# Feed-forward layers: GpSimd makes a block's scale one tile later, and ScalarE makes the shifted copies for the next layer

## The reference, cut to what matters

```python
h = shift_token(x)                     # channels 64..127 come from the token before
q, k, v = jnp.split(h @ wqkv, 3, axis=-1)      # 8 heads of 64
q = l2norm(q) * qs;  k = l2norm(k) * ksc
q, k = rotary_xpos(q, k)
o = local_attention(q, k, v)           # windows of 64, each sees itself and the one before
x = x + o @ wo
h = shift_token(x)
h = (h - h.mean(-1)) / jnp.sqrt(h.var(-1) + 1e-05) * lg + lb
a, g = jnp.split(h @ w1 + b1, 2, axis=-1)
x = x + (a * jax.nn.gelu(g, approximate=False)) @ w2 + b2
```

## Time and profile before

| | |
|---|---|
| median of 3 runs | 1290.07 us (1289.85 to 1290.78) |
| profiled execution, its own time | 1292.57 us |
| its span, first to last instruction | 1290.8 us |
| mean granted TensorE clock | 0.870 |
| busy: TensorE, VectorE, ScalarE, GpSimd | 79%, 60%, 41%, 32% |
| layer 0: attention and feed-forward | about 938 to 1077 us of the span |
| layer 1: projection; attention and feed-forward | about 1077 to 1143; 1145 to 1284 us |

### The profile page before, as it was taken

One profiled execution on the slowest core, in us unless ns is written; L12 is line 12 of the kernel. 1 busy time (PEld: TensorE's weight loads), 2 busy tenths in 40 slices (PEclk: granted clock), 3 DMA queues, 4 the chain that ended last, 5 costly groups with the idle time before them and its releaser, 6 DMA issues.

```text
span 1290.8 us, 20116 instructions
## 1 busy us (share of the span) xinstructions
PE 1026.0 (79%) x7980; PEld 692.3 (54%) x7980; DVE 774.5 (60%) x1349; ACT 529.7 (41%) x1231; POOL 418.0 (32%) x488
## 2 busy tenths in 40 slices
PE   6895876858545189999999777769889789979887
PEld 3563654636423167878787652334456534546643
DVE  2574574654827534646464668969756557956644
ACT  4646555356123311222212060026686514767732
POOL 0724403324106500000000125439843434954420
PEclk9976967669666589999999988979899899979989
DMA  3307135063144374334631210000111210012101
GB/s 94 73 7 143 32 62 109 6 100 71 23 78 197 66 139 98 98 97 75 120 68 29 92 66 1 0 1 0 34 35 39 58 65 26 1 34 51 43 9 33
DMA packets 60479, 76.50 MB, mean 59 GB/s; under 512 B 37500, under 2 KB 41992, under 8 KB 58632
## 3 DMA queue, kind: packets, MB, share of 16 engines
q1 hardware_dynamic: 60396, 75.36, 25.8%
HBM read 52.87 MB, written 1.51 MB: 42 GB/s over the span
## 4 chain that ended last, share of the span: by engine, by line
PE 51%; DVE 16%; POOL 14%; ACT 5%; SPq 5%; DMA 4%; issue 4%; POOLq 0%; DVEq 0%
PE psum L1189 7%; PE psum L1191 6%; PE psum L1190 6%; POOL rest L1426 3%; POOL rest L1416 3%; POOL rest L1422 2%; PE psum L693 2%; PE psum L1670 2%; SPq L1012 2%; POOL rest L1452 2%; DVE main L506 2%; SPq L1018 2%; PE psum L1716 2%; PE psum L1663 2%; DMA rest<-share_d 2%
## 5 line engine op out<-in xcount | busy, mean ns | idle before, releaser
L406 POOL TENSOR_TENSOR kept<-kept 128x8 f32<-128x8 f32 x8 | 1.6, 202 | 401.5 <-DVE kept L383 401.5
L1375 ACT ACTIVATE rest<-psum,main 128x128 f32<-128x128 f32 x256 | 113.3, 482 | 11.6 <-POOL main L1437 8.9
L1036 ACT ACTIVATE x_high<-main 128x512 fp32r<-128x512 f32 x48 | 30.3, 633 | 199.4 <-DVE main L1110 199.4
L1189 PE MATMUL psum<-x_high,w_low 128*128 128x512 f32 x192 | 76.9, 400 | 20.1 <-DVE x_low L1115 20.1
L1452 POOL TENSOR_TENSOR rest<-rest,main 128x512 f32<-128x512 f32 x64 | 65.4, 1042 | 34.6 <-DVE main L1522 34.6
L1189 PE MATMUL psum<-hid_high,w_low 128*128 128x512 f32 x192 | 75.6, 394 | 0.7 <-DVE main L1134 0.7
L1190 PE MATMUL psum<-x_low,w_high 128*128 128x512 f32 x192 | 76.2, 397 | 0.0
L1191 PE MATMUL psum<-x_high,w_high 128*128 128x512 f32 x192 | 76.1, 396 | 0.0
L1190 PE MATMUL psum<-hid_low,w_high 128*128 128x512 f32 x192 | 74.8, 389 | 0.0
L1191 PE MATMUL psum<-hid_high,w_high 128*128 128x512 f32 x192 | 74.7, 389 | 0.0
L1110 DVE TENSOR_TENSOR main<-kept,rest 128x512 f32<-128x512 f32 x48 | 33.1, 690 | 68.1 <-PE psum L1191 43.8
(11 more groups left out here) (316 smaller groups left out, 2841.2 us busy)
## 6 DMA issues: line engine op xcount, KB each, us to landing
rest<-share_d SPq DMA_DIRECT2D x4, 3072.0 KB, 21.4
rest<-share_d SPq DMA_DIRECT2D x4, 2304.0 KB, 20.4
main<-main SPq DMA_DIRECT2D x32, 256.0 KB, 5.2
main<-k_pad SPq DMA_DIRECT2D x16, 512.0 KB, 7.5
rest<-main SPq DMA_DIRECT2D x32, 256.0 KB, 3.5
main<-w_dram SPq DMA_DIRECT2D x2, 3072.0 KB, 14.0
main<-rest SPq DMA_DIRECT2D x32, 128.0 KB, 4.4
rest<-tables_dram SPq DMA_DIRECT2D x2, 2048.0 KB, 8.7
```

What stands on the lines that cost most here:

```text
L1189: T.matmul(dst, w_small, x_large, start=first, stop=False)
L1375: last = A.activation(probs[:, p, 4 * r + m, :], bank[2 * p + r][:, m * P:(m + 1) * P], ACT.Exp, scale=row_scale[:, c, r, m:m + 1], bias=r ...
```

## The change

Two edits, which meet at no semaphore:

- **GpSimd**: `scales(b)` of blocks 0, 1 and 2 is made in iteration 4b+7 in place of 4b+6, behind the weights of tile 4b+7 and the bias of tile 4b+9. Both layers, 6 places. The scale of block 3 stays where it was, at the end.
- **The shifted copies after the feed-forward of layer 0** (4 blocks, 2 copies each and one column of zeros) are made by ScalarE, from a wait on `ff_x`. VectorE's memset becomes a ScalarE copy of a zero column. Blocks 0 and 1 are put between two gelus, one block behind; blocks 2 and 3 stand ahead of ScalarE's first squares of layer 1. VectorE waits for `ff_x` now only in the last layer and once at the end.

```diff
+                def shift(b):
+                    act.wait_ge(sem("ff_x"), L * BLOCKS + b + 1)
+                    first, to = 512 * b, max(512 * b, 1)
+                    if b == 0:
+                        A.activation(sT[HEAD_DIM:P, 0:1], turn_mark[HEAD_DIM:P, 0:1], ACT.Copy)
+                    A.activation(sT[0:HEAD_DIM, first:first + 512], hT[0:HEAD_DIM, first:first + 512], ACT.Copy)
+                    A.activation(sT[HEAD_DIM:P, to:first + 512], hT[HEAD_DIM:P, to - 1:first + 511], ACT.Copy).then_inc(sem("ff_s"), 1)
+
+                more = L + 1 < DEPTH
                 gelu(0, 2)
                 for b in range(1, BLOCKS):
-                    for i in range(N_FF):
-                        gelu(b, i)
+                    gelu(b, 0)
+                    gelu(b, 1)
+                    if more and b >= 2:
+                        shift(b - 2)
+                    gelu(b, 2)
+                if more:
+                    shift(BLOCKS - 2)
+                    shift(BLOCKS - 1)
...
-                if c % 4 == 2 and c > 2:
+                if c % 4 == 3 and c > 3:
                     scales(c // 4 - 1)
...
-                    dve.wait_ge(sem("ff_x"), L * BLOCKS + b + 1)
-                    if L + 1 < DEPTH:
-                        shift(b)
-                    else:
+                    if L + 1 == DEPTH:
+                        dve.wait_ge(sem("ff_x"), L * BLOCKS + b + 1)
                         V.scalar_tensor_tensor(xT[:, sl], hT[:, sl], gate[:, 11:12], xT[:, sl], ALU.mult, ALU.add).then_inc(sem("x_s4"), 1)
...
                 fed(BLOCKS - 1)
+                dve.wait_ge(sem("ff_x"), L * BLOCKS + BLOCKS)
                 dve.sem_inc(sem("ff_w_free"), 1)
```

## The result

The changed kernel takes 1272.01 us, the median of 4 runs (1267.82 to 1273.43); the kernel before takes 1290.42 us in the same comparison (1289.85 to 1295.06, 4 runs). The ratio is 0.9856, 95% interval 0.9831 to 0.988. The forecast was 1268 us, in a range of 1264 to 1276; 18.4 us were gained where 22.1 had been summed up.

What follows compares the result with a forecast made beforehand. No engine is busy throughout; a chain of waits through VectorE, GpSimd and TensorE was taken to bound the stretch changed. Terms 7.5 + 9.6 + 5.3 - 0.3 = 22.1 us, from 1290.07 to 1268 us; range 1264 to 1276.

Steps and rivals of the forecast that it cites:

- tile 7, layer 0 and 1: Attention: earlier weights let the normalisation and TensorE's transposes back come 2.1 us earlier in layer 0, 1.65 in layer 1.
- tile 11, layer 0 and 1: Attention: the gain of tile 7 was to repeat, 2.1 us in layer 0 and 1.65 in layer 1.
- tile 15, layer 0 and 1: Attention: weights 2.6 us earlier and TensorE's clock staying at 2.4 GHz, 4.95 us in layer 0, 4.6 in layer 1.
- copies of block 0: Layer 0's feed-forward: without VectorE's two copies TensorE goes on at once with block 2 at full clock, 5.3 us.
- layer 1 begins later: Block 3: ScalarE's copies delay its first square of layer 1, 0.3 us lost, up to 1.2.
- rival (a): Clock falls anyway: at tile 15 and block 2, 1274 us; at tiles 7 and 11 of layer 0 alone, 1271; chance 0.20.
- The rule against it: Feed-forward copies: VectorE is faster and not saturated, so edit 2 gives nothing or a small loss, sum 17 us.
- Rival (c): Feed-forward: moving copies gains nothing, as GpSimd holds VectorE's next instruction instead; 16.8 us gained, 1273 us; chance 0.08.
- Rival (b): Tiles 7 and 11: the late scale takes back the 7.5 us, leaving 14.6 us gained, 1275.5 us; chance 0.08.
- Rival (d): Six moved scales: 1.2 GHz through two tiles behind each, up to 8 us more per place, 1316 us; chance 0.03.
- Rival (e): Next tile's weights wait for something else the timeline hides: no measurable effect, 1290 us; chance 0.03.
- the two signs of being wrong: Attention: the normalisation does not start earlier, or stretches at clock 0.50 stand behind the scales.

Runs made afterwards that it cites:

- the normalisation first: Changed kernel with GpSimd's scale ahead of the bias and, at tiles 7 and 11, VectorE's normalisation ahead of copies and reciprocal: 1265.24 us.
- the scores first: Changed kernel with TensorE's transposes back of blocks 0 and 1 one step later, behind the scores of tile 10 (14): 1257.9 us.
- tables-later: Kernel before, with GpSimd's four products on the tables held back until block 0's copies are done: ratio 0.9981.
- copies alone: Kernel before with only the shifted copies moved to ScalarE, the scales left in their old place: ratio 0.9976.
- late at tile 15 alone: Changed kernel with the scales of blocks 0 and 1 back at tiles 6 and 10, block 2's still late: ratio 0.9891 to the kernel before.

## Why the prediction was right

By the ruler, term by term, in us gained:

| term | forecast | measured |
|---|---|---|
| tile 7, layer 0 and 1 | 2.1 + 1.65 | 2.10 + 1.65 |
| tile 11, layer 0 and 1 | 2.1 + 1.65 | 0.53 + 0.08 |
| tile 15, layer 0 and 1 | 4.95 + 4.6 | 5.10 + 5.38 |
| copies of block 0 | 5.3 | 5.37 |
| layer 1 begins later | -0.3 | -0.37 |
| sum | 22.1 | 19.8 |

- **The mechanism** was as told: the weights start behind their reciprocal, and TensorE's wait moves to the transposes back and is 1.9 to 2.0 us long (2 had been said). Waits for the weights fell to 5.8 us (6 said).
- **Tile 11 is the step that failed.** "Tile 11 repeats it" took for granted that the clock there would be as at tile 7. It fell behind the new wait, and 1.57 us went in each layer: the size that rival (a) had put on one fall (1.6), at places that it named only for layer 0. With one such fall in each layer the sum would have been 18.9 us. The two runs that shorten the wait give this loss back: in layer 0 the normalisation first gains 1.6 us more at tile 11 than at tile 7, the scores first 2.2 us more. Over tiles 7 and 11 of both layers in all ten profiles, the clock fell at 19 of the 28 waits of 1.9 to 2.3 us and at none of the 12 waits under 1 us. It fell at none of the 14 waits of 1.25 us at tile 15 either. So in these runs the fall came with the long wait alone, but not with every long wait; why the same wait at tile 7 does no harm stays open.
- **Tile 15** gave 0.9 us more than reckoned, 0.78 of it in layer 1. Of these, 0.63 had been gained before r14: behind it TensorE came to its next values (L1693, below) after 1.91 us in layer 1 and after 2.54 us in layer 0 (r14 is at 1214.21 and 1013.56 us). At tile 11 the fall began 0.9 us behind the wait in layer 1 and 0.2 us behind it in layer 0, and TensorE got through its work there 0.65 us faster. The reciprocal r14, on VectorE, stood 10.0 us behind the wait in both layers, so the ruler counts this gain one stage late. The clock stayed at 2.4 GHz through the gate matmuls, as I had taken; without that it would have been 5.2 us in all.

```profile
1016.10 0.34 PE L1693 MATMUL psum<-rest 128*64 128x64 f32 x4
...
1216.12 0.34 PE L1693 MATMUL psum<-rest 128*64 128x64 f32 x4
```

- **Edit 2**: the copy on ScalarE took 0.63 us, the value chosen between 0.63 and 1.08. The rule against it, to keep what VectorE does faster, would have had no gain; the tables-later run shows why it does not hold here. A copy that takes 0.42 us alone takes 2.5 beside GpSimd. Rival (c) is out: no VectorE instruction was held in the copies' place.
- **Rival (b)**, the late scale, did decide at tiles 7 and 11, by 0.26 to 0.29 us, and took nothing back. **Rival (d)**, two tiles at half clock behind each scale, did not come: the stretches behind tiles 11 in the change are under 4 us long, and there is none behind tiles 7. Its argument read the stretch at tile 15 as 6.0 us; that was the length of the window, and the granted clock was 0.50 for 6.8 us, from 1026.8 to 1033.6. **Rival (e)**, no effect, is out. Of the two signs of being wrong that were named, one came in part: stretches at half clock do stand behind the scale at both tiles 11.
- The median lies 4.0 us above the forecast, at the very edge of the "within 4 us" that had 0.55, and nearer to the 1271 us of rival (a)'s second case. The terms above account for 2.3 us of it; the rest is less than the first 940 us vary from one profile to the next. The range held because it had room for some falls of the clock, not because the falls at tile 11 had been foreseen.

## What to carry to other kernels

When a small step is moved behind a big one on an in-order queue, ask where the wait goes, and whether the waiting engine has other work that could stand ahead of it: the change shortened TensorE's waits, and giving TensorE its next scores first made an end of it, for another 11.6 us. A wait of TensorE costs its length and, as at tile 11 here, it can cost a half-speed stretch behind it (1.6 us). A small VectorE copy from SBUF to SBUF beside long GpSimd products cost about a product each here (2.5 us in place of 0.42), so move such a copy to ScalarE or out of their way.

## What the runs showed of the hardware

- The clock fell behind waits of 1.9 us at one place and not at another, the same way in two profiles of the same kernel; behind waits of 0.9 and 0.26 us at the same places it did not fall. Layer 1 of the kernel before had fewer falls than layer 0 for the same work, and lost that when earlier stages became 5 to 10 us shorter (copies alone, late at tile 15 alone), but not when they became 3.6 us shorter (the tables later: 23.74 us for tile 7). So a stage that an edit does not touch can come out up to 0.8 us longer (24.55 us for 23.75); what decides it is not shown.
- VectorE and GpSimd do not share a loss evenly: before, two copies lost 2 x 2.1 us, and GpSimd's four products 0.35 us in all.
- Execution times of this kernel scatter by 0.5% and more, and the part up to r0 alone varied by 10 us over ten profiles. Of the 2.4 us between the two profiles of the change, 1.9 lay there. Stages cut from the traces mostly tell 0.1 us.
